# Routed experts over scattered slot tiles in DRAM in a transformer block on one Trainium2 core

## The chip, the core and the metric

The kernel runs on one NeuronCore of one Trainium2 chip. The metric is the device time of one execution in microseconds. Engines are named as the profile names them: PE is TensorE (PEld its weight loads), DVE is VectorE, ACT is ScalarE, POOL is GpSimd, SP is SyncE, whose queue issues the DMAs.

## What is computed

x has 8 sequences of 512 tokens of 128 channels, all float32. The block is attention and a mixture of experts, both on layer-normalised input and both added to x. The attention has 16 heads of 8 channels, is causal, and adds relative terms to keys and values; it isn't touched. The expert part is, cut to what matters:

```
scores = softmax(xt @ gate_w.T)                 # 4096 tokens, 8 experts
idx = top_k(scores + gate_bias, 2)
weights = scores at idx
y = 0
for e in range(8):
    gate_e = sum(where(idx == e, weights, 0))
    h = silu(xt @ w1[e].T) * (xt @ w3[e].T)     # 128 -> 128
    y = y + gate_e[:, None] * (h @ w2[e].T)
z = silu(xt @ sw1.T) * (xt @ sw3.T) @ sw2.T     # shared, 128 -> 256 -> 128
x = x + y + z
```

## The kernel before

The program of each engine is written out by hand, with semaphores between them; an engine runs its instructions strictly in their written order.

**Attention** takes two thirds of the time. It goes over 16 pieces e (group g of two sequences, row i of 128 queries; the rows of a group in the order 2, 0, 1, 3) and 8 quads of heads q in each, as units m in software-pipelined slots. Relative scores go through DRAM: rel_copy (L974) leaves them in relS, SP's put_rel (L689) writes them to w_slots, get_near (L697) reads them back skewed into the ring near, and DVE's scores_min (L1075) adds them; exp (L998), the transposes tp (L849), their copies on ACT (L987) and DVE (L1060), and the products av follow. POOL's near_probs (L791 to L799) makes the near probabilities. For each piece there follow rv (products with tv, L882), near_values, yt (transposes, L890), normalise, yb, pj and residual; store (L711) writes the result x1 to x1_dram. The last piece's rv, yt, yb and pj run in last_row, between the first steps of the expert stage; the text calls this the tail.

**The expert stage** (expert_part) has 8 chunks of 512 tokens, one for each sequence, and 10 steps in each: two shared halves and eight experts, each over all 512 tokens. A step on TensorE is hidden (L1357 and L1358: two products of 128x512 with w1 and w3 into h1_ps and h3_ps) and product for the step two before (L1367: four products of 128x128 with the tokens' hidden values hT as weights and w2 moving; eight for the shared pair). ACT's Silu (L1392) reads h1_ps, DVE's L1412 multiplies it with h3_ps into hT. DVE adds the product to acc: L1420 for the shared part, with x1, and four L1427 for an expert, scaled by the token's gate. The gates of a token that did not choose the expert are zero, and two of the eight experts are chosen for each token, so six of eight products are multiplied by zero.

During one chunk the next is prepared: normalise on ACT (L1267), four transposes on TensorE (L1275), their copy (L1282), gate scores on TensorE (L1290), and on DVE and ACT the softmax and the choice of two (gates_shift, gates_softmax, gates_pick, gates_write; about twenty small operations, each of which waits for the one before). SP loads the chunk (L1224) and stores the output of each (L1233). The weights of all ten experts come in five DMAs during attention's third group, three chunks of x1 at the start of the last piece.

## Time and profile before

| | |
|---|---|
| three timed runs | 773.13, 774.75, 775.63 us; median 774.75 |
| span of the profiled execution | 770.0 us; no other time of its own is given for it |
| granted TensorE clock, mean | 0.979 |
| busy share of the span | PE 90%, DVE 77%, ACT 67%, POOL 33% |
| attention and projections | until about 540 us |
| expert stage | from 540.1 us to the end |

A row of the groups of instructions gives the line, the engine, the operation, out<-in by name, the shape, the count, then busy time and the mean duration of one. Matmuls overlap, so the pitch between them is read from the timeline. A float32 matmul is two records, a transpose one.

### The profile page before, as it was taken

The page shows a single profiled execution, that of the slowest core. Times are in us where ns is not written, and L with a number is a line of the kernel's source. Part 1 is how long each engine was busy: PE and PEld are TensorE (multiplying, and loading weights), DVE is VectorE, ACT ScalarE, POOL GpSimd, SP SyncE. Part 2 cuts the span into 40 slices and gives each one's busy share as a digit, 9 for nine tenths or more (in the row PEclk, how much of TensorE's full clock was granted, in tenths as well). Part 3 has the DMA queues.
Part 4 walks back from the last instruction along what each step waited for, and adds up shares of the span by engine and source line. Part 5 has one row for each costly group of instructions (what it writes and reads, how often), then busy time and mean ns, then how long its engine had stood idle before and what let it go on. Part 6 is the DMA issues. An engine that isn't in the chain of part 4 may idle for free. (4 is left out here: it accounts for less than half of the span.)

```text
span 770.0 us, 27094 instructions
## 1 busy us (share of the span) xinstructions
PE 690.5 (90%) x10316; PEld 507.9 (66%) x10368; DVE 589.2 (77%) x2036; ACT 514.7 (67%) x1032; POOL 255.8 (33%) x253
## 2 busy tenths in 40 slices
PE   4687879899888899988999988988999999999997
PEld 3465657677666677766777766766666666666665
DVE  7965686788787788787888887977566776677676
ACT  3686967688797878888888998887335343443331
POOL 9443445334355534545543445533000000000000
PEclk9988989999999999999999999999999999999999
DMA  9899998689989778787778779841000000000000
GB/s 255 262 295 335 333 303 264 203 244 277 309 250 302 255 222 253 249 238 241 236 222 266 221 232 255 271 153 50 3 22 28 29 5 23 28 15 1 14 15 14
DMA packets 117839, 138.48 MB, mean 180 GB/s; under 512 B 8976, under 2 KB 86288, under 8 KB 117520
## 3 DMA queue, kind: packets, MB, share of 16 engines
q1 hardware_dynamic: 117712, 136.75, 58.6%
q8 instruction: 84, 1.38, 0.8%
q14 instruction: 43, 0.35, 0.1%
HBM read 82.26 MB, written 54.46 MB: 178 GB/s over the span
## 5 line engine op out<-in xcount | busy, mean ns | idle before, releaser
L1075 DVE CUSTOM_DVE_ANT_0 ps<-ps,near 128x128 f32<-128x128 f32 (+3 forms) x512 | 245.1, 509 | 90.5 <-PE ps L837 57.0
L998 ACT ACTIVATE work<-ps,nmin 128x128 f32<-128x128 f32 (+3 forms) x512 | 248.4, 548 | 54.2 <-DVE nmin L1075 49.4
L849 PE MATMUL ps<-ident,work 128*128 128x128 f32 x1280 | 202.6, 278 | 20.7 <-issue 11.6
L849 PEld LDWEIGHTS ps<-ident,work 128*128 128x128 f32 x1280 | 157.0, 143 | 36.5 <-issue 13.7
L795 POOL TENSOR_SCALAR_AFFINE_SELECT work<-work 128x512 f32<-128x512 f32 x96 | 61.5, 641 | 237.8 <-ACT work L987 203.6
L1392 ACT ACTIVATE near<-ps 128x512 f32<-128x512 f32 x80 | 47.5, 595 | 133.3 <-PE ps L1357 133.2
L799 POOL TENSOR_TENSOR work<-work 128x512 f32<-128x512 f32 x96 | 124.2, 1294 | 8.0
L1060 DVE COPY work<-ps 128x512 f32<-128x512 f32 (+1 forms) x192 | 123.2, 642 | 2.5 <-issue 1.6
L837 PE MATMUL ps<-kb,qb 128*128 128x384 bf16 (+3 forms) x460 | 110.6, 298 | 12.3 <-ACT work L998 9.4
L1367 PEld LDWEIGHTS ps<-work,near 128*128 128x128 f32 x640 | 82.6, 192 | 34.2 <-issue 31.6
L987 ACT ACTIVATE work<-ps 128x512 f32<-128x512 f32 (+1 forms) x160 | 90.2, 564 | 18.7 <-PE ps L849 18.1
L866 PE MATMUL ps<-work,vb 128*9 128x128 f32 x2560 | 96.1, 277 | 4.2 <-ACT relS L974 2.6
L1412 DVE TENSOR_TENSOR near<-near,ps 128x512 f32<-128x512 f32 x80 | 54.9, 687 | 50.3 <-ACT near L1392 36.4
L974 ACT ACTIVATE relS<-ps 128x512 f32<-128x512 f32 x128 | 84.4, 660 | 11.6 <-PE ps L824 10.2
L1367 PE MATMUL ps<-work,near 128*128 128x128 f32 x640 | 83.2, 275 | 0.0
L1357 PE MATMUL ps<-near,work 128*128 128x512 f32 x160 | 82.8, 599 | 0.0
L1358 PE MATMUL ps<-near,work 128*128 128x512 f32 x160 | 81.8, 593 | 0.0
L1427 DVE SCALAR_TENSOR_TENSOR near<-ps,near 128x128 f32<-128x128 f32 x256 | 71.9, 343 | 5.3
L866 PEld LDWEIGHTS ps<-work,vb 128*9 128x9 f32 x2560 | 57.7, 91 | 26.5 <-issue 19.7
L1075 DVE DVE_READ_ACCUMULATOR2_ANT nmin<- 128x1 f32 x512 | 72.1, 141 | 0.0
L882 PE MATMUL ps<-tv,work 128*32 128x8 f32 x4096 | 59.3, 179 | 12.1 <-issue 11.9
L882 PEld LDWEIGHTS ps<-tv,work 128*32 128x32 f32 x4096 | 48.2, 112 | 30.5 <-issue 27.3
(111 smaller groups left out, 627.3 us busy)
## 6 DMA issues: line engine op xcount, KB each, us to landing
near<-w_slots SPq DMA_DIRECT2D x96, 512.0 KB, 5.4
w_slots<-relS SPq DMA_DIRECT2D x128, 256.0 KB, 4.5
qk_rows<-work SPq DMA_DIRECT2D x36, 256.0 KB, 4.7
near<-w_slots SPq DMA_DIRECT2D x32, 256.0 KB, 4.6
qk_rows<-y SPq DMA_DIRECT2D x9, 256.0 KB, 6.8
qb<-qk_rows SPq DMA_DIRECT2D x24, 96.0 KB
kb<-qk_rows SPq DMA_DIRECT2D x24, 96.0 KB
qb<-qk_rows SPq DMA_DIRECT2D x48, 48.0 KB
```

What stands on the lines that cost most here:

```text
L799: nc.gpsimd.tensor_tensor(dst, ptmp[:, :, :], pT[:, q % 2, :, i * P:(i + 1) * P], ALU.add).then_inc(pc_done, 1)
L837: ins = nc.tensor.matmul(qk_ps[:, m % 3, h * wide:(h + 1) * wide], qb[:, n, i * P:(i + 1) * P], kb[:, n // 4 * 2 + n % 2, 0:wide], start=T ...
L849: ins = nc.tensor.transpose(tp_ps[:, m % 2, n * P:(n + 1) * P], prob[:, m % PROBS, n * P:(n + 1) * P], ident[:, :])
L866: ins = nc.tensor.matmul(bank[32 * h:32 * h + VD, a * P:(a + 1) * P], vb[:, g % 2, b * NI + j, n * VD:(n + 1) * VD], pT[:, q % 2, h, j * P ...
L882: ins = nc.tensor.matmul(bank[32 * tq:32 * tq + NH, a * D:(a + 1) * D], pcT[:, e % 2, tau, :], tv[:, tau, :], start=True, stop=True)
L974: nc.scalar.activation(relS[:, q % RSLOTS, :, :, :].rearrange("p a j h -> p a h j"), misc("rel", q).rearrange("p (a h j) -> p a h j", a=2, ...
L987: nc.scalar.activation(pT[:, q % 2, n * w:n * (w + 1), 0:wide], tp_ps[:, m % 2, 0:n * wide].rearrange("p (h s) -> p h s", h=n), ACT.Copy). ...
L998: ins = nc.scalar.activation(prob[:, m % PROBS, h * wide:(h + 1) * wide], qk_ps[:, m % 3, h * wide:(h + 1) * wide], ACT.Exp, bias=nmin[:, ...
L1060: nc.vector.tensor_copy(pT[:, q % 2, n * w:n * (w + 1), 0:wide], tp_ps[:, m % 2, 0:n * wide].rearrange("p (h s) -> p h s", h=n)).then_inc( ...
L1075: nc.vector.tensor_tensor_reduce(out=scores, in0=scores, in1=near[:, q % NEAR, a, 4 * P - wide:4 * P, r], scale=1.0, scalar=3e38, op0=ALU. ...
L1357: nc.tensor.matmul(h1_ps[k % 2], w1_sb[:, m, :], rhs, start=True, stop=True).then_inc(h1_ready, 1)
L1367: ins = nc.tensor.matmul(y_ps[k % 2][:, n * P:(n + 1) * P], hT[:, (NM * c + m) % 4, n * P:(n + 1) * P], w2_sb[:, m, :], start=(m == ms[0]) ...
```

## The change

The expert stage is written anew; attention itself stays. The tokens are four batches of 8 tiles (1024 tokens). For each batch DVE counts, with a scan and two small matmuls on TensorE (prefix), how many tokens go to each expert, rounds each expert's count up to whole tiles of 128 slots (gates_place), and so has the slot of each token for each of its two experts (pos) and the expert of each slot tile (emap). A batch has at most RT = 23 slot tiles, whatever the routing, so 92 are always computed, in 24 rounds of up to four (six rounds a batch, the last of three).

- GpSimd, whose program had ended with attention, scatters: 64 indirect DMAs, each of 128 normalised rows (512 B each) of a tile, into xs_dram; and later 64 gathers of the same size from ys_dram into yg. All scatters stand before all gathers in its queue.
- SP clears xs_dram before (24 DMAs of up to 256 KB in the last attention row), loads the slots of each round (load_slots), stores its products (store_slots), and stores the output at the very end.
- TensorE runs the 16 shared steps of all chunks first (FRONT = CHUNKS), with the chunks' transposes and gate scores between them, and then the 24 rounds: transposes of the slots (turn_slots), for each tile a product with w1 and w3 of its own expert, and the product with w2.
- ACT reads four experts' numbers into registers in each round and copies these experts' weights (384 columns a tile) into wbuf, and copies each product from PSUM to yo (take_product).
- DVE copies the turned slots (copy_slots), and in combine multiplies the gathered rows by the token's weight and adds them, four operations for two tiles; eight lots in steps 30 to 39, eight after the loop.
- The tail of the last piece uses one PSUM bank, and the residual comes one step sooner. Weights come in eight DMAs, chunks 2 to 5 after the last near load.

The core of the diff:

```diff
+CT = CH // P
+CHUNKS = TILES // CT
+
+BATCHES = 4
+BT = TILES // BATCHES
+RT = (TOPK * BT * P + E * (P - 1)) // P
+ROUND = 4
+ROUNDS = -(-RT // ROUND)
+NR = BATCHES * ROUNDS
+CLEARS = NR
+ZEROS = C
+RED = 3 + 2 * TOPK
+RSET = 6 * BT * E + (TOPK + 1) * BT * E + RED * BT + 7 * E + RT * (E - 1)
+NTAB = 2 * P + E * BT + RT + E
+WSETS = 4
+XGS = 6
+YOS = 3
+YGS = 4
+FRONT = CHUNKS
+SEQ = ([("shared", c, m) for c in range(FRONT) for m in range(NSH)] + [("round", r, 0) for r in range(NR)]
+       + [("shared", c, m) for c in range(FRONT, CHUNKS) for m in range(NSH)])
+NS = len(SEQ)
+ROUND_AT = NSH * FRONT
+TURN_AT = [-1, 0, 1, 2, 3, 4, 9, 10]
+GATE_AT = [0] + [at + 1 for at in TURN_AT[1:]]
+PREFIX_AT = [5, 7, 9, 15]
+PICKS_AT = [(1, 2, 2, 3, 4), (3, 4, 5, 6, 6), (5, 6, 7, 8, 8), (11, 12, 12, 13, 14)]
+COMBINE_AT = [*range(30, 34), *range(36, 40)]
...
 RSLOTS = 5
...
 PROBS = 5
-WEIGHTS = 5
+WEIGHTS = 8
 MINS = 32
...
-                        for j in range(3):
+                        for j in range(2):
+                            wait_stored(sp, j)
+                            experts["load"](sp, j)
+                    if 0 <= m - FIRST[NQ - QUADS] - 2 < CLEARS:
+                        experts["clear"](sp, m - FIRST[NQ - QUADS] - 2)
+                    if m == READ_AT[NQ - 1] + 1:
+                        for j in range(2, CHUNKS - 2):
                             wait_stored(sp, j)
                             experts["load"](sp, j)
                 load_residual(GI - 1)
...
-                        experts["pool"](pool)
+                        experts["pool_start"](pool)
                     near_probs(q)
+                experts["pool"](pool)
...
+    def clear_slots(sp, k):
+
+        sp.wait_ge(zero_done, 1)
+        g, n = divmod(k, ROUNDS)
+        a = tiles_of(k)
+        sp.dma_start(xs_dram[g][n * ROUND * P:(n * ROUND + a) * P, :].rearrange("(p a) c -> p a c", p=P),
+                     zeros.unsqueeze(1).broadcast_to([P, a, C])
+        ).then_inc(zero_out, 16)
+
     def load_tokens(sp, j):
-        sp.dma_start(x1c[j % 3], x1_tiles[:, CT * j:CT * (j + 1), :]).then_inc(x1c_in[j % 3], 16)
...
+    def load_slots(sp, r):
+
+        g, n = divmod(r, ROUNDS)
+        if n == 0:
+            sp.wait_ge(xs_out[g], 16 * TOPK * BT)
+        wait(sp, xg_ready, r - XGS + 1)
+        sp.dma_start(xg[:, r % XGS, 0:tiles_of(r), :], slot_rows(xs_dram, r)).then_inc(xg_in[r % XGS], 16)
+
+    def store_slots(sp, r):
+
+        sp.wait_ge(yo_done, r + 1)
+        sp.dma_start(slot_rows(ys_dram, r), yo[:, r % YOS, 0:tiles_of(r) * C].rearrange("p (a c) -> p a c", c=C)
+                     ).then_inc(yo_out[r % YOS], 16)
 
     def sync_program(sp, wait_stored):
+        for j in range(CHUNKS - 2, CHUNKS):
+            wait_stored(sp, j)
+            load_tokens(sp, j)
+        for r in range(XGS):
+            load_slots(sp, r)
+        for r in range(NR):
+            store_slots(sp, r)
+            if r + XGS < NR:
+                load_slots(sp, r + XGS)
         for c in range(CHUNKS):
-            if c + 3 < CHUNKS:
-                sp.wait_ge(acc_done, AC * c + 1)
-                wait_stored(sp, c + 3)
-                load_tokens(sp, c + 3)
-            sp.wait_ge(acc_done, AC * (c + 1))
-            sp.dma_start(out_tiles[:, CT * c:CT * (c + 1), :], acc[:, c % 2, :, :]).then_inc(out_done[c % 2], 16)
-        for n in range(2):
-            sp.wait_ge(out_done[n], 16 * CHUNKS // 2)
+            sp.wait_ge(comb_done, TOPK * CT * (c + 1))
+            sp.dma_start(out_tiles[:, CT * c:CT * (c + 1), :], x1c[c]).then_inc(out_done, 16)
+        sp.wait_ge(out_done, 16 * CHUNKS)
+
+    def pool_start(pool):
...
     def pool_program(pool):
-        for e in range(E):
-            ins = nc.gpsimd.memset(order[:, e:e + 1], float(E - e))
-        ins.then_inc(order_done, 1)
+        pool.wait_ge(zero_out, 16 * CLEARS)
+        for g in range(BATCHES):
+            pool.wait_ge(pos_done, g + 1)
+            pool.wait_ge(xn_done, BT // CT * (g + 1))
+            for n in range(BT):
+                for r in range(TOPK):
+                    c, m = divmod(g * BT + n, CT)
+                    nc.gpsimd.indirect_dma_start(
+                        xs_dram[g], bass.IndirectOffsetOnAxis(pos[:, g, r, n:n + 1], 0), xn[:, c, m, :], None,
+                        bounds_check=RT * P - 1, oob_is_err=False).then_inc(xs_out[g], 16)
+        for g in range(BATCHES):
+            for k in range(YOS):
+                pool.wait_ge(yo_out[k], 16 * len(range(k, ROUNDS * (g + 1), YOS)))
+            for n in range(BT):
+                lot = (g * BT + n) // 2
+                if n % 2 == 0:
+                    wait(pool, comb_done, TOPK * 2 * (lot - YGS + 1))
+                for r in range(TOPK):
+                    nc.gpsimd.indirect_dma_start(
+                        yg[:, lot % YGS, n % 2, r, :], None, ys_dram[g],
+                        bass.IndirectOffsetOnAxis(pos[:, g, r, n:n + 1], 0),
+                        bounds_check=RT * P - 1, oob_is_err=False).then_inc(yg_in[lot % YGS], 16)
...
+    def turn_slots(pe, r):
+        pe.wait_ge(xg_in[r % XGS], 16 * (r // XGS + 1))
+        wait_turned(pe, "slots", r)
+        for a in range(tiles_of(r)):
+            ins = nc.tensor.transpose(xT_ps[:, a * P:(a + 1) * P], xg[:, r % XGS, a, :], t["ident"][:, :])
+        ins.then_inc(xg_ready, 1)
...
+    def prefix(pe, g):
+
+        pe.wait_ge(count_done, g + 1)
+        pe.wait_ge(*((sh_done, 2), (sh_done, 3), (cnt_done, 2), (sh_done, 4))[g])
+        totals = routes[g % 2]["count_by_expert"][:, :, BT - 1]
+        nc.tensor.matmul(cnt_ps[:, 0:E], before, totals, start=True, stop=True)
+        nc.tensor.matmul(cnt_ps[:, E:2 * E], ones, totals, start=True, stop=True).then_inc(cnt_ready, 1)
...
+    def gates_count(dve, g):
+
+        v, then = routes[g % 2], chained(dve, g, 16)
+        pick = v["pick"]
+        then(nc.vector.tensor_tensor(v["mine_by_expert"].rearrange("p e n -> p n e"), pick[:, 0, :, :], pick[:, 1, :, :], ALU.add))
+        nc.vector.tensor_tensor_scan(v["count"], keep, v["mine"], 0.0, ALU.mult, ALU.add).then_inc(count_done, 1)
+
+    def gates_place(dve, g):
+
+        v, then = routes[g % 2], chained(dve, g, 17)
+        cnt, pad, off, tmp = v["cnt"], v["pad"], v["off"], v["tmp"]
+        dve.wait_ge(cnt_ready, g + 1)
+        nc.vector.tensor_copy(cnt, cnt_ps).then_inc(cnt_done, 1)
+        dve.wait_ge(cnt_done, g + 1)
+        then(nc.vector.tensor_scalar(pad[:, 0, :], cnt[:, E:2 * E], float(P - 1), None, ALU.add))
+        then(nc.vector.tensor_scalar(pad[:, 1, :], pad[:, 0, :], 7, 7, ALU.logical_shift_right, ALU.logical_shift_left))
+        then(nc.vector.tensor_tensor_scan(v["last"], ones[:, 0:E], pad[:, 1, :], 0.0, ALU.mult, ALU.add))
+        then(nc.vector.tensor_tensor(off[:, 0, :], cnt[:, 0:E], v["last"], ALU.add))
+        then(nc.vector.scalar_tensor_tensor(out=off[:, 1, :], in0=off[:, 0, :], scalar=-1.0,
+                                            in1=pad[:, 1, :], op0=ALU.add, op1=ALU.subtract))
+        then(nc.vector.tensor_tensor(v["rank_by_expert"], v["count_by_expert"],
+                                     off[:, 1, :].unsqueeze(2).to_broadcast([P, E, BT]), ALU.add))
+        for r in range(TOPK):
+            then(nc.vector.tensor_tensor(tmp[:, :, :], v["pick"][:, r, :, :], v["rank_by_expert"].rearrange("p e n -> p n e"),
+                                         ALU.mult))
+            with nc.allow_low_precision(reason="numbers of slots are whole"):
+                ins = nc.vector.tensor_reduce(pos[:, g, r, :], tmp[:, :, :], AX.X, ALU.add)
+            if r + 1 < TOPK:
...
+    def gates_map(dve, g):
+
+        v, then = routes[g % 2], chained(dve, g, 26)
+        wide7 = [P, RT, E - 1]
+        then(nc.vector.tensor_tensor(v["eq"], starts.unsqueeze(2).to_broadcast(wide7),
+                                     v["last"][:, 0:E - 1].unsqueeze(1).to_broadcast(wide7), ALU.is_ge))
+        with nc.allow_low_precision(reason="numbers of experts are whole"):
+            nc.vector.tensor_reduce(emap[:, g, 0:RT], v["eq"], AX.X, ALU.add).then_inc(emap_done, 1)
+        for r in range(TOPK):
+            then(nc.vector.tensor_tensor(v["tmp"][:, :, :], v["pick"][:, r, :, :], v["score"][:, :, :], ALU.mult))
...
+        def hidden(s):
+            kind, n, m = SEQ[s]
+            wait(pe, silu_done, s - 1)
+            wait(pe, hT_done, s - 1)
+            if kind == "shared":
+                pe.wait_ge(xnT_done, n + 1)
+                nc.tensor.matmul(h1_ps[s % 2], ws[:, 0, m, :], xnT[:, n, :], start=True, stop=True).then_inc(h1_ready, 1)
+                nc.tensor.matmul(h3_ps[s % 2], ws[:, 1, m, :], xnT[:, n, :], start=True, stop=True).then_inc(h3_ready, 1)
+                return
+            pe.wait_ge(xgT_done, n + 1)
+            pe.wait_ge(wbuf_done, n + 1)
+            for k, (bank, ready) in enumerate(((h1_ps, h1_ready), (h3_ps, h3_ready))):
+                for a in range(tiles_of(n)):
+                    at = slice(a * P, (a + 1) * P)
+                    ins = nc.tensor.matmul(bank[s % 2][:, at], wbuf[:, n % WSETS, a, k * P:(k + 1) * P], xgT[:, n % 2, at],
+                                           start=True, stop=True)
+                ins.then_inc(ready, 1)
+
...
+                for a in range(CT):
+                    for k in range(NSH):
+                        ins = nc.tensor.matmul(bank[:, a * P:(a + 1) * P], hT[:, (s - 1 + k) % 4, a * P:(a + 1) * P],
+                                               ws[:, 2, k, :], start=(k == 0), stop=(k == NSH - 1))
+            else:
+                for a in range(tiles_of(n)):
+                    ins = nc.tensor.matmul(bank[:, a * P:(a + 1) * P], hT[:, s % 4, a * P:(a + 1) * P],
+                                           wbuf[:, n % WSETS, a, 2 * P:3 * P], start=True, stop=True)
             ins.then_inc(y_ready, 1)
 
...
-            if k == NM * (CHUNKS - 4):
+        def copy_weights(r):
+            g, n = divmod(r, ROUNDS)
+            if n == 0:
+                act.wait_ge(emap_done, g + 1)
+            at = slice(ROUND * n, ROUND * n + tiles_of(r))
+            _, which = nc.values_load_multi_w_load_instructions(
+                emap[0:1, g, at], engines=[mybir.EngineType.Activation], min_val=0, max_val=E - 1,
+                skip_runtime_bounds_check_because="a count of seven comparisons")
+            if r >= WSETS:
+                act.wait_ge(y_ready, made(ROUND_AT + r - WSETS))
+            for a in range(tiles_of(r)):
+                ins = nc.scalar.activation(wbuf[:, r % WSETS, a, :], wr_v[:, bass.ds(which[a] * W, W)], ACT.Copy)
+            ins.then_inc(wbuf_done, 1)
+
+        def take_product(s):
+            r, p = SEQ[s][1], PRODUCTS.index(s)
+            act.wait_ge(y_ready, p + 1)
+            wait(act, yo_out[r % YOS], 16 * (r // YOS))
+            nc.scalar.activation(yo[:, r % YOS, 0:tiles_of(r) * C], y_bank(p)[:, 0:tiles_of(r) * C], ACT.Copy
+                                 ).then_inc(yo_done, 1)
...
+                cut = P * tiles_of(SEQ[s][1]) if SEQ[s][0] == "round" else CH
+                act.wait_ge(h1_ready, s + 1)
+                wait(act, hT_done, s - 1)
+                nc.scalar.activation(silu[:, s % 2, 0:cut], h1_ps[s % 2][:, 0:cut], ACT.Silu).then_inc(silu_done, 1)
+            last_row(s)
+            if s >= 2 and SEQ[s - 2][0] == "round":
+                take_product(s - 2)
+            if s + 2 < NS and SEQ[s + 2][0] == "round":
+                copy_weights(SEQ[s + 2][1])
+            for j in range(1, CHUNKS):
+                if TURN_AT[j] == s:
+                    copy_turned(act, j)
...
+        def copy_slots(r):
+            cut = P * tiles_of(r)
+            dve.wait_ge(xg_ready, r + 1)
+            if r >= 2:
+                dve.wait_ge(h3_ready, ROUND_AT + r - 1)
+            nc.vector.tensor_copy(xgT[:, r % 2, 0:cut], xT_ps[:, 0:cut]).then_inc(xgT_done, 1)
...
+        def add_shared(s):
+            c, p = SEQ[s][1], PRODUCTS.index(s)
+            dve.wait_ge(y_ready, p + 1)
+            nc.vector.tensor_tensor(x1c[c], y_bank(p).rearrange("p (n c) -> p n c", c=C), x1c[c], ALU.add).then_inc(acc_done, 1)
+
+        def combine(lot):
+            g, n = divmod(2 * lot, BT)
+            c, m = divmod(2 * lot, CT)
+            dve.wait_ge(acc_done, c + 1)
+            dve.wait_ge(yg_in[lot % YGS], 16 * 2 * TOPK * (lot // YGS + 1))
+            for r in range(TOPK):
+                for k in range(2):
+                    if r:
+                        dve.wait_ge(comb_done, 2 * TOPK * lot + k + 1)
+                    nc.vector.scalar_tensor_tensor(out=x1c[c][:, m + k, :], in0=yg[:, lot % YGS, k, r, :],
+                                                   scalar=wsel[:, g, r, n + k:n + k + 1], in1=x1c[c][:, m + k, :],
+                                                   op0=ALU.mult, op1=ALU.add).then_inc(comb_done, 1)
```

## Rows read from the trace of the kernel before

**Rows 1.** The page: busy share of each engine, and DMA by slices.

```profile
PE 690.5 (90%) x10316; PEld 507.9 (66%) x10368; DVE 589.2 (77%) x2036; ACT 514.7 (67%) x1032; POOL 255.8 (33%) x253
...
DMA  9899998689989778787778779841000000000000
```

**Rows 2.** Busy time by windows: length, then each engine, clock, DMA share, GB/s.

```profile
485.00:500.00 15.00, 14.36 (x320) 11.18 (x322) 13.47 (x45) 13.80 (x29) 8.00 (x10) 1.00 0.82 261
500.00:515.00 15.00, 12.35 (x284) 9.81 (x287) 10.68 (x33) 12.05 (x20) 4.86 (x6) 1.00 0.52 173
515.00:530.00 15.00, 14.08 (x270) 11.33 (x276) 13.88 (x42) 12.21 (x21) 5.84 (x7) 1.00 0.27 82
...
575.00:602.43 27.43, 27.43 (x134) 17.86 (x133) 20.77 (x73) 13.46 (x21) 0.00 (x0) 1.00 0.07 20
```

**Rows 3.** The page: the chain that ended last, shares by line.

```profile
PE ps L1367 9%; PE ps L1357 9%; PE ps L1358 9%; PE ps L1290 1%; PE ps L1275 1%; PE ps L882 0%; PE ps L866 0%; DVE near L1427 0%; ACT work L987 0%; PE ps L849 0%; ACT near L1267 0%; PE ps L905 0%; PE ps L890 0%; ACT work L998 0%; PE ps L837 0%
```

**Rows 4.** Timeline of TensorE within a chunk: start, length, instructions.

```profile
607.53 1.95 PE L1367 MATMUL ps<-work,near 128*128 128x128 f32 x16
609.32 0.60 PE L1275 MATMUL ps<-ident,near 128*128 128x128 f32 x4
609.75 1.02 PE L1357 MATMUL ps<-near,work 128*128 128x512 f32 x2
610.62 1.02 PE L1358 MATMUL ps<-near,work 128*128 128x512 f32 x2
611.47 1.05 PE L1367 MATMUL ps<-work,near 128*128 128x128 f32 x8
612.37 1.02 PE L1357 MATMUL ps<-near,work 128*128 128x512 f32 x2
```

**Rows 5.** Timeline: first and last matmul of the stage, last store.

```profile
540.10 1.13 PE L1357 MATMUL ps<-near,work 128*128 128x512 f32 x2
...
765.78 0.28 PE L1367 MATMUL ps<-work,near 128*128 128x128 f32 x1
767.25 0.37 SPq L1233 DMA_DIRECT2D out<-near  x1
```

**Rows 6.** Groups of instructions of ScalarE, by form.

```profile
L1392 ACT ACTIVATE near<-ps 128x512 f32<-128x512 f32 x80 | 47.5, 595 | 133.3 <-PE ps L1357 133.2
L987 ACT ACTIVATE work<-ps 128x384 f32<-128x384 f32 x64 | 32.8, 513 | 3.5 <-PE ps L849 3.5
```

**Rows 7.** Timeline of VectorE and ScalarE, 602 to 607 us.

```profile
602.28 1.12 DVE L1427 SCALAR_TENSOR_TENSOR near<-ps,near 128x128 f32<-128x128 f32 x4
...
603.53 0.19 DVE L1335 TENSOR_TENSOR near<-near 128x32 f32<-128x32 f32 x1
603.76 0.19 DVE L1336 TENSOR_TENSOR near<-near,work 128x32 f32<-128x32 f32 x1
...
605.65 1.64 ACT L1267 ACTIVATE near<-vb,work,rstd 128x128 f32<-128x128 f32 x4
```

**Rows 8.** One line's instructions: SP's output stores, issue and landing.

```profile
L1233 SPq DMA_DIRECT2D out<-near x8: 372/378/378, 578.0 to 767.2; - x8
...
DMA to landing us min/median/max: 2.3/2.3/2.9
```

**Rows 9.** The page: groups of instructions, GpSimd and VectorE at 128x512.

```profile
L795 POOL TENSOR_SCALAR_AFFINE_SELECT work<-work 128x512 f32<-128x512 f32 x96 | 61.5, 641 | 237.8 <-ACT work L987 203.6
...
L799 POOL TENSOR_TENSOR work<-work 128x512 f32<-128x512 f32 x96 | 124.2, 1294 | 8.0
L1060 DVE COPY work<-ps 128x512 f32<-128x512 f32 (+1 forms) x192 | 123.2, 642 | 2.5 <-issue 1.6
```

**Rows 10.** Timeline of SP's queue in the last attention row.

```profile
494.03 0.53 SPq L697 DMA_DIRECT2D near<-w_slots  x1
...
518.97 0.53 SPq L697 DMA_DIRECT2D near<-w_slots  x1
```

**Rows 11.** The page: DMA issues, KB each, us to landing.

```profile
near<-w_slots SPq DMA_DIRECT2D x96, 512.0 KB, 5.4
```

More of the change, by code:

```diff
@@ L9 @@
 BF16 = mybir.dt.bfloat16
+I32 = mybir.dt.int32
 ALU = mybir.AluOpType
@@ L39 @@
 CH = 512
+CT = CH // P
[25 more added lines that the diff above has]
+COMBINE_AT = [*range(30, 34), *range(36, 40)]
+TURNED = [("turn", 0)]
+for s in range(NS):
+    if s + 1 < NS and SEQ[s + 1][0] == "round":
+        TURNED.append(("slots", SEQ[s + 1][1]))
+    if s in TURN_AT:
+        TURNED.append(("turn", TURN_AT.index(s)))
+PRODUCTS = [s for s in range(NS) if SEQ[s][0] == "round" or SEQ[s][2] == NSH - 1]
 GI = G * NI
@@ L1207, in prepared_at, with tiles_of @@
-    def prepared_at(j):
-        late = LATE if j == 1 else 0
-        base = NM * (j - 1) + late
-        return {"normalise": base - late + 1, "turn": base + 2, "copy": base + 3, "scores": base + 4, "shift": base + 5,
-                "exp": base + 6, "softmax": base + 7, "pick0": base + (8 if j > 1 else 7),
-                "pick1": base + (9 if j > 1 else 8)}
-    def due(step, what):
-        return [j for j in range(1, CHUNKS) if prepared_at(j)[what] == step]
+    def tiles_of(r):
+        return min(ROUND, RT - ROUND * (r % ROUNDS))
@@ L1508, in twice @@
         return placed
-    hidden = lambda shared, experts: np.concatenate([shared.reshape(NSH, P, C), experts]).transpose(2, 0, 1)
+    tables = np.concatenate([np.broadcast_to(row, (P, row.shape[-1])) for row in (
+        np.triu(np.ones((P, P), np.float32), 1), np.ones((1, P), np.float32),
+        np.tile((np.arange(BT) > 0).astype(np.float32), E)[None], P * np.arange(RT, dtype=np.float32)[None],
+        E - np.arange(E, dtype=np.float32)[None])], axis=1)
     arrays = {
```

426 lines of the change are left out of this document (221 added, 205 removed).

## Prediction

> **What bounds the kernel now.** I read the page first: TensorE is busy for 90% of the span, more than any other engine, and in the slices the DMA engines fall nearly silent for the last 30% of the span [rows 1]. Then the busy time by windows: in the expert stage, from 540.1 us on, TensorE is busy without a gap (27.43 us of 27.43 in one chunk of ten steps) at full granted clock, with ScalarE at 13.5 us, VectorE at 20.8 us, GpSimd at nothing and DMA at 7% [rows 2]. The chain of waits says the same: its expert part is the three matmul lines alone [rows 3]. So that stage is worth what TensorE's work in it is worth, and nothing else in it is near a limit. Last I read the pitch of the matmuls from the timeline, since a matmul's own duration (593 ns) overlaps its successor's: one 128x512 product is two records and 0.855 us (611.47 less 610.62), a group of four 128x128 products with new weights each is eight records and 0.89 us (0.2225 each), the double group of a shared product 1.79, four transposes 0.43 us [rows 4]. Twenty hidden products, one shared and eight routed second products and four transposes are 17.1 + 1.79 + 7.12 + 0.43 = 26.4 us; the other 1.0 us of a chunk's 27.43 is its gate scores.
>
> The profiled execution is given with its span of 770.0 us alone; the timed runs' median of 774.75 lies 4.75 us above it. I make the sum against the span, and add 4.75.
>
> **What the change takes from TensorE.** The stage has 80 hidden steps now, and its last matmul ends at 766.1 [rows 5]: 226.0 us. Of it 80 x 1.71 = 136.8 are hidden products, 64 x 0.89 = 57.0 routed second products, 8 x 1.79 = 14.3 shared ones, 3.0 and 8.0 transposes and gate scores. The rest, 6.9 us, is the last attention row's tail (rv, yt, yb, pj) with its waits; it stays, now in one PSUM bank. Afterwards the shared part is 16 x 1.71 + 14.3 + 11.0 = 52.7, with the tail 59.6, and with eight small prefix matmuls (0.2 each) and a stall or two some 62 us. A slot tile costs three 128x128 products with new weights and a transpose: 3 x 0.2225 + 0.108 = 0.775 us, 92 tiles 71.3 us. TensorE's work falls from 226 to 133 us. That is the most that can come back, 93 us; the question is what else now takes over 133 us.
>
> **ScalarE in the rounds.** Each of 24 rounds (20 of four tiles, 4 of three) asks of it a Silu of 0.595 us and a PSUM copy of the same size; four copies of 384 columns into wbuf, 513 ns each from the nearest form [rows 6], with 0.10 us of each hidden under the next (four L1267 of 0.48 us take 1.64 us together) [rows 7]: 3 x 0.416 + 0.513 = 1.76; and a load of four expert numbers from SBUF into registers, which no row shows. Below it is nothing (behind Silu and copy); above, the shortest round trip to memory in the trace, a store's 2.3 us from issue to landing [rows 8]. I take 1.1, near the middle, since nothing says which end is nearer. A round is then 0.60 + 0.60 + 1.76 + 1.1 = 4.05 us (3.4 with three tiles), against TensorE's 3.1, so ScalarE sets the pace: 20 x 4.05 + 4 x 3.4 = 94.6 us. With the ends it is 3.1 (TensorE's) to 5.3. VectorE needs 0.64 us for copy_slots [rows 9], about as much for the gated product and at most 1.12 for a combine a round [rows 7] and is covered. TensorE at three quarters busy should keep its clock: the window 500 to 515, 82% busy, has 1.00 [rows 2].
>
> **GpSimd's queue.** It is idle now from 541 on. It gets 64 scatters and then 64 gathers, each of 128 rows of 512 B, one instruction each, strictly in order. None is in the trace. Bound from below: SP hands a DMA out in 0.38 us [rows 8]. Above: 2.3 us, if each held the queue until it landed. GpSimd's own 128x512 instructions take 0.64 to 1.29 us [rows 9]. With 128 addresses to work out I take 1.2 us, near GpSimd's dearer instruction and below the landing. The Trainium skill, "DMA: Bandwidth & Descriptors", section "Anatomy of one DMA", gives a GpSimd-issued DMA about 2.0 us fixed, most of it the completion, not the setup. Held in the queue for the whole of it, 128 would be 256 us and the span some 833; no row here shows which part holds the queue.
>
> When can it start? The first batch's positions come after the prefix at step 5. Steps 0 to 4 cost TensorE 5 x 1.71 + 1.79 + 5 x 1.25 = 16.6 us plus some 6 of the tail, step 5 some 4, then eleven chained VectorE operations at 0.225 us each (603.53 to 603.76) [rows 7]: 30 us after 540.1. The chain of 36 such operations a batch is 8.1 us, 32 for four; with 16 gated products, 8 additions (0.65 to 0.7 each) and some 4 us of tail that is 53 of the 62 us, so covered, if closely. Scatters run from 30 to 30 + 64 x 1.2 = 107; batch 0's land at about 52, before the first round's transposes at 58. Gathers of the first three batches follow without a gap (their rounds are stored by 97, 121, 145), and the last 16 start at 164.
>
> **The sum.** Last round: 62 + 94.6 + 3 for the two steps behind = 160; stored and landed 2.7 later, 162.3. GpSimd comes free for the last batch at 30 + 112 x 1.2 = 164.4, so its queue decides, by 2 us. Sixteen gathers, 19.2: 183.6. Behind the last: 2.3 to land, 1.12 for its four VectorE products, 0.4 and 2.3 for the last store: 6.1, so 189.7. 540.1 + 189.7 = 729.8.
>
> **The clears and the loads.** SP issues 24 clears of 256 KB during the last attention row, 493 to some 527, 6 MB where the DMA engines are 82, 52 and 27% busy [rows 2]. Five near loads (512 KB, 5.4 us to landing) go out between them in SP's queue, the last at 518.97 [rows 10, 11], and VectorE's scores wait for those, ScalarE's exp for VectorE, TensorE's transposes for that. The idle DMA share of 493 to 527 is some 17 us' worth of all engines; 5.9 MB at 261 / 0.82 = 318 GB/s is 19. So some contention is left: I take 1 us, with nothing and 6 us as ends (nothing, if the loads stay ahead; 6, if all five land 1.2 us late, one clear's issue and transfer each). Weights go from five DMAs to eight, of 0.4 to 0.5 us on SP, some 0.2 MB more, spread over 14 units two rows earlier: on a queue whose DMAs wait for ScalarE's rel copies anyway: nothing. Chunks 2 to 5 are loaded at once behind the last near load, under the end of attention; the two last chunks behind the last store as now. The batched gate takes four exponentials and their table loads from ScalarE, which is not what sets the end there. Span 731, time **736 us**, 5% faster.
>
> **Rivals.**
> - *The last gathers are cheap and registers too (faster still).* At 0.9 us a DMA and 3.4 us a round: 62 + 80 + 3 + 2.7 + 14.4 + 6.1 = 168, 713 us. For it: a 64 KB DMA is little work. With both lower ends, 0.38 and 3.1, it is 151, 696 us.
> - *GpSimd's queue is the bound and eats the gain (slower).* The end is 540.1 + 30 + 128c + 6.1 + 1, equal to today's 770 at c = 1.51 us. At 1.75 it is 801, 806 us; at 2.3 it is 872, 876. For it: 128 rows need 128 addresses each way and the queue is serial; GpSimd needs 1.29 us for one tensor addition [rows 9]. Against: SP's 0.38. This is the rival that ends on the other side, and one price decides it.
> - *Register loads hold ScalarE.* The end is 62 + 24 x r + 3 + 2.7 + 19.2 + 6.1 + 1, equal to today's at r = 5.7 us a round, a load of 2.7 us; four single loads in a row would do that. At 6.5 us a round it is 790, 795 us. The Trainium skill, "DMA: Bandwidth & Descriptors", section "Latency and other measured facts", gives a register load a floor of about 600 ns; by that a round would be 3.6 us and the sum, set by GpSimd, the same.
> - *VectorE locks GpSimd out.* If every copy_slots (0.64 us) held the descriptors back, 24 of them would add 15 us: 751 us. The Trainium skill, "SBUF — State Buffer", has this for fp32 copies from SBUF to SBUF in a fast mode. Against: these read PSUM, and L1060's 512 columns from PSUM take 0.642 us [rows 9], so no fast mode shows.
>
> **Chances.** Forecast (722 to 755 us) 0.50, with VectorE's lock in it; both cheap 0.15; GpSimd over 1.5 us a DMA 0.21; registers 0.08; something between, near no change or a little under, 0.06. The break-even is only a quarter above my price for a DMA that no row shows, so the range must reach over: 708 (0.8 us a DMA, 3.3 a round) to 800 (1.7 us a DMA); the likeliest case alone 722 to 755. Faster by over 0.3% 0.69, within 0.3% (about what a measurement of this kernel can tell from no change) 0.03, slower 0.28.
>
> **What would show it.** TensorE busy some 135 us behind 540, not 226. Rounds at an even pitch of some 4.05 us, with ScalarE named before TensorE's hidden products (wbuf); at 3.1 the register load is hidden. On GpSimd 128 DMAs at a pitch of 1.2 us, the first some 570, with no gap between scatter and gather but at batch ends. The last 16 gathers with TensorE silent for 20 to 25 us at the end. Attention's end within 2 us of where it was. Wrong it would be by a pitch over 1.5 us on GpSimd, by ScalarE rounds over 5.7 us, or by near loads that land late.

## The result, and the profile of the changed kernel

The changed kernel takes 828.72 us (median of 4 runs, 825.82 to 837.52), the kernel before 773.94 in runs beside it: ratio 1.074, 95% interval 1.066 to 1.081. Forecast were 736 us and a range of 708 to 800; the prediction was wrong. The same kernel, unaltered, ran again later, on chip 3, with the experiments below: 753.86 us (two runs) against 771.44 there, ratio 0.976 (0.966 to 0.985). Both are results of this change. Most of this text is about what lies between them.

The page of the first run, for rows 1 and 3 (engines, slices, then the chain by engine):

```profile
PE 633.3 (77%) x10260; PEld 493.0 (60%) x10260; DVE 528.0 (64%) x1820; ACT 533.5 (65%) x1098; POOL 383.9 (47%) x374
...
PEclk9988899999999999999999999999758869796955
DMA  9899998799997797786877989901231024353352
...
another core or an unknown queue 10%; PE 7%; DVE 5%; issue 4%; ACT 3%; POOL 1%; DMA 1%; POOLq 0%; ACTq 0%; DVEq 0%
```

TensorE's work has fallen as meant, 690.5 to 633.3 us [rows 1], but the span has grown to 825.5 and the first name in the chain is no engine of the kernel: a release that the profile can't place. This is one core, so there is no other core to wait for. Its windows, for rows 2 (length, busy of PE, PEld, DVE, ACT, POOL, then clock, DMA share, GB/s):

```profile
500.00:515.00 15.00, 14.10 (x294) 10.63 (x291) 11.72 (x37) 13.01 (x21) 4.73 (x5) 1.00 1.07 322
515.00:530.00 15.00, 14.66 (x269) 11.56 (x268) 13.18 (x38) 12.07 (x21) 5.79 (x6) 1.00 1.06 306
575.00:602.43 27.43, 11.63 (x50) 7.17 (x48) 13.90 (x55) 8.32 (x13) 20.73 (x23) 0.75 0.34 103
```

The clears fill the DMA engines (share 1.07), and TensorE is as busy there as before: 14.10 and 14.66 us of 15, against 12.35 and 14.08. Behind the first scatter, which starts at 574.05, it is busy for 11.63 us of 27.43, at a mean granted clock of 0.75. The timeline of all engines shows why:

```profile
587.62 0.22 DVE L1485 TENSOR_REDUCE near<-near 128x8 f32<-128x64 f32 x1 [0.21 <-DVE near L1535]
589.02 0.23 DVE L1486 TENSOR_TENSOR near<-near 128x64 f32<-128x64 f32 x1 [1.18 <-DVE near L1485]
589.72 0.23 DVE L1487 TENSOR_TENSOR near<-near,work 128x64 f32<-128x64 f32 x1 [0.47 <-DVE near L1486]
...
603.22 1.09 PE L1405 MATMUL ps<-ident,near 128*128 128x128 f32 x4
604.10 1.92 PE L1544 MATMUL ps<-near,work 128*128 128x512 f32 x2
605.81 1.18 PE L1545 MATMUL ps<-near,work 128*128 128x512 f32 x2
613.87 0.97 POOL L1350 DMA_INDIRECT xs_dram<-near  x1 [0.30 <-issue]
619.12 0.69 DVE L1661 TENSOR_TENSOR relS<-ps,relS 128x512 f32<-128x512 f32 x1 [17.34 <-remote]
619.24 0.60 ACT L1410 ACTIVATE near<-ps 128x512 f32<-128x512 f32 x1 [32.38 <-remote]
```

L1410 copies what L1405's four transposes wrote. They end at 604.3; the copy starts at 619.24. In between ScalarE does nothing, and nothing else that the copy needs is under way. So 14.9 us of its 32.38 idle are a late signal; the rest is before the transposes ended. VectorE's chained operations wait only on VectorE's own signals, and stand 0.7 to 1.4 us apart where they took 0.23 [rows 7]. No instruction of ScalarE or VectorE got longer (0.60, 0.69, 0.22 us as ever); TensorE's did only with the clock (1.92 us for L1544's two where 1.02 is usual). I read it as a late signal from one instruction to the next. GpSimd's line in the same stretch is a run of scatters 1.28 us apart; its last begins at 613.87, and 4.4 us after that ends (614.8) the waiters go.

### The profile page after: what moved, and what is told of

The parts are those of the page before. It is cut to its first block and busy times, and to the rows that moved or that the text cites. A ratio compares the mean times of both kernels' runs of the same rounds, so it can differ in the third digit from the quotient of the medians.

```text
span 825.5 us, 27095 instructions
## 1 busy us (share of the span) xinstructions
PE 633.3 (77%) x10260; PEld 493.0 (60%) x10260; DVE 528.0 (64%) x1820; ACT 533.5 (65%) x1098; POOL 383.9 (47%) x374
## 5 line engine op out<-in xcount | busy, mean ns | idle before, releaser
L880 PE MATMUL ps<-kb,qb 128*128 128x128 bf16 (+3 forms) x512 | 130.8, 307 | 11.9 <-ACT work L1036 9.0
L1361 POOL DMA_INDIRECT work<-ys_dram,near x64 | 66.1, 1033 | 75.9 <-DMA ys_dram<-work 25.4
L1025 ACT ACTIVATE work<-ps 128x512 f32<-128x512 f32 (+1 forms) x160 | 90.4, 565 | 15.5 <-PE ps L892 14.9
L1350 POOL DMA_INDIRECT xs_dram<-near x64 | 62.4, 976 | 69.7 <-DVE near L1520 51.2
L1012 ACT ACTIVATE relS<-ps 128x512 f32<-128x512 f32 x128 | 84.3, 660 | 11.1 <-PE ps L867 9.5
L1552 PE MATMUL ps<-kb,qb 128*128 128x128 f32 x368 | 54.2, 308 | 40.0 <-DVE kb L1647 23.5
L1552 PEld LDWEIGHTS ps<-kb,qb 128*128 128x128 f32 x368 | 49.8, 217 | 43.9 <-issue 43.0
L925 PE MATMUL ps<-tv,work 128*32 128x8 f32 x4096 | 58.7, 179 | 11.6 <-issue 11.5
L1647 DVE COPY kb<-ps 128x512 f32<-128x512 f32 (+1 forms) x24 | 16.0, 668 | 78.1 <-remote 41.2
L880 PEld LDWEIGHTS ps<-kb,qb 128*128 128x128 bf16 x512 | 40.5, 98 | 31.9 <-ACT work L1036 16.2
L867 PE MATMUL ps<-te,qb 128*128 128x128 bf16 x512 | 50.5, 222 | 6.2 <-ACT relS L1012 5.5
```

The costliest lines, as they stand in the source:

```text
L880: ins = nc.tensor.matmul(qk_ps[:, m % 3, h * wide:(h + 1) * wide], qb[:, n, i * P:(i + 1) * P], kb[:, n // 4 * 2 + n % 2, 0:wide], start=T ...
L925: ins = nc.tensor.matmul(bank[32 * tq:32 * tq + NH, a * D:(a + 1) * D], pcT[:, e % 2, tau, :], tv[:, tau, :], start=True, stop=True)
L1012: nc.scalar.activation(relS[:, q % RSLOTS, :, :, :].rearrange("p a j h -> p a h j"), misc("rel", q).rearrange("p (a h j) -> p a h j", a=2, ...
L1025: nc.scalar.activation(pT[:, q % 2, n * w:n * (w + 1), 0:wide], tp_ps[:, m % 2, 0:n * wide].rearrange("p (h s) -> p h s", h=n), ACT.Copy). ...
L1361: nc.gpsimd.indirect_dma_start(yg[:, lot % YGS, n % 2, r, :], None, ys_dram[g], bass.IndirectOffsetOnAxis(pos[:, g, r, n:n + 1], 0), bound ...
L1552: ins = nc.tensor.matmul(bank[s % 2][:, at], wbuf[:, n % WSETS, a, k * P:(k + 1) * P], xgT[:, n % 2, at], start=True, stop=True)
```

## Experiments

Each ran beside the kernel before, on one chip for each group of runs. The runs name the chip: 10 for the first four, 11 for the second four, then 0, 3 and 8, in this order of time. The first result above has no chip named. "Remote" is the profile's word for a wait whose release it can't place. The kernel before has some too, 14 of at most 1.8 us in attention (11.9 us in all); what is said of remote waits below is of the expert stage.

**Without any DMA of GpSimd.** The loops of L1350 and L1361 are gone; the combine reads zeros.

> The changed kernel with all 128 DMAs of GpSimd left out (no scatter, no gather: the slot tiles hold the zeros of the clears, the combine reads zeros; the output is not the reference's). Slot loads wait for the clears and for shared step 12 alone. Theory A (the DMAs that GpSimd issues back to back hold back the other engines' signals): with them gone, the 16 shared steps run from 540 in about 62 us, the 24 rounds follow at the undisturbed pitch of 3.45 us (83 us), the combine and stores add about 12: span 695 to 715. Rival B (the rounds themselves are dear: a register load on ScalarE, 368-column copies, PE's many small matmuls): rounds stay above 4.5 us and the span is above 740. Rival C (the slot loads and stores on SP's queue are the wait): the waits on xg loads stay and the span is above 780.

Measured: 713.55 us, ratio 0.928 (0.921 to 0.934), no remote wait. The span, 710.8, lies in Theory A's range; rivals B and C fall. With all 24 rounds in it, the rest of the change is worth 58 us.

**A probe in the kernel before.** Behind GpSimd's last attention work, from step 5 of the expert stage:

```
+        for n in range(64):
+            nc.gpsimd.indirect_dma_start(flat[:, n * P:(n + 1) * P], None, rows,
+                bass.IndirectOffsetOnAxis(at, 0), ...).then_inc(probe_in, 16)
```

> The kernel before, with 64 indirect gathers of 128 rows of 512 bytes added on GpSimd, from step 5 of the expert stage on, back to back, to an unused part of the work tile; nothing waits for them. Theory A: after some ten of them the expert steps of TensorE, ScalarE and VectorE pause until the burst of about 64 x 1.3 = 83 us has ended: 30 to 75 us slower than before, with idle time put down to a remote or unknown releaser. Rival (the wait comes from the changed kernel's own order of work, or from slot traffic): within 3 us of before, since the idle GpSimd has 190 us for it.

Measured: 845.57 us against 771.51, ratio 1.099 (1.092 to 1.107). ScalarE's timeline:

```profile
611.53 0.60 ACT L1406 ACTIVATE near<-ps 128x512 f32<-128x512 f32 x1 [18.57 <-remote]
662.63 0.60 ACT L1406 ACTIVATE near<-ps 128x512 f32<-128x512 f32 x1 [50.50 <-remote]
664.17 0.60 ACT L1406 ACTIVATE near<-ps 128x512 f32<-128x512 f32 x1 [0.95 <-remote]
```

The gathers run from 574.0 to 657.4. ScalarE's instruction at 662.63 reads what this product wrote, in TensorE's timeline:

```profile
619.10 1.92 PE L1371 MATMUL ps<-near,work 128*128 128x512 f32 x2
```

It ended at 621.0, 41.6 us before its reader started. Nothing in the kernel waits for the probe, and yet it costs 74 of the 83 us that it lasts. A lack of instructions is an unlikely cause: the two queues that the profile calls instruction moved no packet between 600 and 664, so ScalarE's instruction at 662.63 hadn't just been fetched.

**The same with plain DMAs.** `dma_start(flat[...], rows[0:P, :])`, also 64 KB and from GpSimd.

> The same probe with 64 plain 64 KB loads issued by GpSimd instead of indirect ones. If issuing from GpSimd in itself (its software queue) is what holds signals back, 20 to 75 us slower than before; if it takes the indirection, within 3 us of before.

Measured: 773.74 us, ratio 1.000 (0.995 to 1.004), on the same chip. They stand 0.53 us apart. So issuing from GpSimd isn't enough; of these two it takes the indirect form.

**The changed kernel, spaced.** Two waited memsets behind each indirect DMA:

```
+                    for _ in range(2):
+                        nc.gpsimd.memset(zeros, 0.0).then_inc(zero_done, 1)
+                        spent[0] += 1
+                        pool.wait_ge(zero_done, spent[0])
```

> The changed kernel with two waited memsets of 128 x 128 on GpSimd behind each of its 128 DMAs, which should widen their pitch from 1.28 to about 1.9 us. Theory A with a backlog (signals pass when the DMAs come slower than they are served, some 1.4 us each): the pauses of 12 to 32 us vanish, rounds run at 3.5 to 4 us, and the end is set by GpSimd's own queue, 574 + 128 x 1.9 = 817 and about 15 behind it: span 820 to 850. Theory A without a threshold (any run of such DMAs holds signals back until it pauses): the pauses grow with the queue, span above 880.

Measured: 876.14 us, ratio 1.139. The pitch came out at 2.25 us, (864.8 - 579.2) / 127, not 1.9, and there is no remote wait in the trace, on the chip on which the probe had 119 us of them. So the pauses vanished, as the theory with a backlog had it, and the span of 875.9 came out above its 820 to 850, because the pitch did; the sum below explains it.

**Pitch, rows, bursts, payload.** Four variants of the probe: one waited memset behind each; 32 rows in place of 128; a wait for all landings after each eight; rows of 64 bytes.

> The probe of 64 indirect gathers in the kernel before, with one waited memset of 128 x 128 behind each, which should set their pitch at about 1.75 us (574 to 686). Backlog theory (each such DMA leaves work behind GpSimd that takes about as long as, or a little longer than, its 1.3 us of issue, and signals pass once it is given time): nearly no loss, under 10 us over before. Theory without a threshold (each DMA costs the other engines some 1.2 us of held signals whatever its pitch): again 60 to 85 us over before.

> 64 indirect gathers of 32 rows instead of 128, back to back. If the held signals come from the number of descriptors (rows), the loss is under 15 us, and the issue time shows how much of the 1.0 us on GpSimd is for the rows and how much is fixed; if it is the indirect DMA as such, the loss is the length of the burst again, over 40 us.

> The probe of 64 indirect gathers in bursts of 8, GpSimd waiting after each burst until all of it has landed (about 2 us). Backlog theory: signals are held only within a burst and pass at its end, so single pauses stay under 10 us and the loss is under 30 us where the unbroken burst lost 74. Without a backlog that empties in those 2 us the loss is 60 us or more.

> 64 indirect gathers of 128 rows of 64 bytes instead of 512, back to back: an eighth of the payload with the same descriptors. If the payload's traffic holds the signals, the loss falls under 15 us; if the descriptors do, it stays at 60 to 85 us over before.

| | pitch, us | time, us | ratio |
|---|---|---|---|
| one memset | 2.00 | 772.80 | 0.999 (0.995 to 1.004) |
| 32 rows | 1.22 | 846.67 | 1.096 (1.084 to 1.107) |
| bursts of 8 | 1.30, then a 2.2 us pause | 786.77 | 1.018 (1.007 to 1.030) |
| 64 bytes a row | 1.30 | 850.74 | 1.101 (1.089 to 1.113) |

Neither the number of rows nor the payload matters: 32 rows cost GpSimd 0.91 us against 1.00 and hold the others as long. The pauses between DMAs do: at 2.00 us nothing is lost. Bursts of eight lose about 14. Between 1.30 and 2.00 us no pitch was tried, and each pause came with a wait of GpSimd (on a memset, or on landings), so distance and wait aren't told apart. There is no run of this changed kernel at 1.3 us on chips 10 or 11.

**The changed kernel at that pitch, and without its gathers.**

> The changed kernel with one waited memset behind each of its 128 indirect DMAs, so that they stand 2.0 us apart, the pitch at which the probe lost nothing. If the held signals were all that made the change slow, the span comes near 713 plus a few us. If the queue itself then bounds, its last gather ends at about 574 + 128 x 2.0 = 830 and the span is 838 to 850, with TensorE no longer waiting on remote releasers but on slot loads and on the combine.

Measured: 838.58 us, ratio 1.087, on chip 0; the queue's end is the bound, as the second sentence had it. As no run on that chip showed late signals, paced or not, this one doesn't test whether the pitch protects from them.

> The changed kernel without its 64 gathers (the combine reads zeros, so the output is not the reference's); the scatters stand back to back as before. Backlog theory: the pauses of 12 to 17 us up to 677 stay, the rounds after them run undisturbed at 3.45 us, span 740 to 765, so that scatters and gathers cost about 40 and 70 us of the 115 over the run without either. If the scatters are harmless and only gathers hurt, the span is within 8 us of 713.

Measured: 709.20 us, ratio 0.920 (0.912 to 0.927). By its number this is the second expectation, harmless scatters. But in the first trace signals were late while scatters alone ran, so neither reading fits both: here the 64 scatters stand in one unbroken run of 82 us at 1.28 us, at the same point of the same program as in the first trace, and no signal is late. My backlog theory had no room for this. What differed was the program behind that point, or the chip.

**The same programs on one chip.**

> The changed kernel unaltered, beside the three runs below on one chip. Its first trace shows pauses of 12 to 32 us on remote releasers from the twelfth scatter on; the run without gathers, on another chip, shows none in the same instructions up to that point. If the chip makes the difference, this run goes with the other three: all four with such pauses (828 us here) or none (about 765 to 790 here). If the programs do, it is 820 to 840 with pauses while the next but one has none.

> The kernel before with 64 indirect gathers back to back, once more. If the chip makes the difference it follows the changed kernel: 845 us where that shows pauses, near the kernel before where it doesn't. If the programs do, 845 us again whatever the others show.

> The changed kernel without its gathers, once more (the combine reads zeros, the output is not the reference's). If the programs make the difference, 709 us again with no remote waits though its 64 scatters stand in an unbroken run of 82 us; if the chip does and this is one that holds signals, 735 to 765.

Measured, on chip 3: 753.86, 771.52 (ratio 1.000, 0.995 to 1.004) and 710.40 us. No remote wait in the expert stage of any. The changed kernel came out under even the 765 to 790 expected of it without pauses. The probe's windows on chip 10, and then on chip 3:

```profile
600.00:620.00 20.00, 5.21 (x14) 2.86 (x13) 1.81 (x5) 0.60 (x1) 15.15 (x16) 0.59 0.16 49
640.00:660.00 20.00, 0.00 (x0) 0.00 (x0) 0.00 (x0) 0.00 (x0) 13.40 (x14) 0.50 0.15 46
```

```profile
600.00:620.00 20.00, 20.00 (x98) 13.09 (x97) 13.75 (x45) 6.08 (x13) 15.16 (x16) 1.00 0.25 77
640.00:660.00 20.00, 20.00 (x98) 13.07 (x97) 15.11 (x54) 8.48 (x12) 13.28 (x14) 1.00 0.17 55
```

One program, the same 14 to 16 DMAs on GpSimd in each stretch, and TensorE at nothing (and half clock) or at everything. The program alone isn't the cause; the chip, or a state that it was in, decides. The changed kernel on chip 3, one window of the rounds:

```profile
640.00:700.00 60.00, 57.73 (x484) 54.95 (x483) 28.75 (x61) 47.85 (x105) 45.98 (x47) 1.00 0.69 197
```

Its scatters and gathers (lengths in ns, then first and last start; then what GpSimd waited for ahead of the gathers, us and times):

```profile
L1350 POOL DMA_INDIRECT xs_dram<-near x64: 971/972/1209, 576.2 to 656.9; - x64
...
L1361 POOL DMA_INDIRECT work<-ys_dram,near x64: 992/997/1082, 658.2 to 740.8; - x64
its engine sat idle before it (us, times) until:
  issue: 17.7, 58
  DMA ys_dram<-work: 0.9, 3
  DVE relS L1672: 0.9, 3
```

And TensorE's last round, in its timeline:

```profile
699.97 1.58 PE L1552 MATMUL ps<-kb,qb 128*128 128x128 f32 x12
```

TensorE's last round starts at 699.97; the gathers go on to 741.8 and the span ends at 751.3. GpSimd waits for others for less than 3 us from 576.2 on (1.8 ahead of gathers, 0.3 ahead of scatters). Its queue is the bound here.

**Half of the tokens dense.** What the runs pointed to: take half of the DMAs away, and put dense work where GpSimd was waited for. Batches 0 and 1 stay with slot tiles (12 rounds, 32 scatters, 32 gathers), the chunks of batches 2 and 3 go through all eight experts, and these steps stand around the rounds:

```
+MIX = "D" * 8 + "RRDRRDRRDD" + "RRDRRDRRD" + "D" * 17
+            if kind == "dense":
+                rhs = xnT[:, n, :]
...
+                nc.tensor.matmul(h1_ps[s % 2], wr_v[:, m * W:m * W + P], rhs, ...)
+                nc.tensor.matmul(h3_ps[s % 2], wr_v[:, m * W + P:m * W + 2 * P], rhs, ...)
...
+                nc.vector.scalar_tensor_tensor(out=x1c[c][:, a, :], in0=y[:, a, :], scalar=routes[g % 2]["lg"][:, n + a, e:e + 1],
+                                               in1=x1c[c][:, a, :], ...)
```

> A mixture: routed experts over slot tiles for the first half of the tokens alone (32 scatters and 32 gathers, 12 rounds), all eight experts on all rows for the other half as before the change (32 dense steps), these placed around the rounds, and the indirect DMAs 2.0 us apart. Work of TensorE: 62 us for the shared steps, 32 x 2.7 = 86, 12 x 3.45 = 41, so an end near 540 + 189 = 729; the queue ends near 574 + 32 x 2.0, then 650 + 32 x 2.0 = 716, in front of that. Span 725 to 740, some 40 us under the kernel before. If held signals need more than this pitch, or if the queue's waits land in VectorE's order, 750 or more.

> The same mixture with its indirect DMAs back to back (1.3 us apart) in bursts of 16 to 32. Backlog theory: the 32 scatters hold signals from about the tenth on and cost 10 to 30 us, the gathers in two bursts of 16 another 5 to 15: span 745 to 775, 15 to 45 us over the paced one. If pacing doesn't matter, the two are within 3 us.

Measured on chip 0: paced 735.19 us, ratio 0.954 (0.945 to 0.962); unpaced 738.59, ratio 0.959 (0.953 to 0.964); the 745 to 775 that the backlog theory gave the unpaced one didn't come. The unpaced one on chip 3, beside the changed kernel:

> The half-and-half mixture without pacing, once more: 738 us if the programs make the difference or if this chip holds no signals; 750 to 780, with remote waits in the bursts, if the chip does and holds them.

737.35 us, ratio 0.954, where the changed kernel had 753.86. Once more both, on chip 8:

> The half-and-half mixture with its indirect DMAs 2.0 us apart, on another chip. If the chip is one on which runs of indirect DMAs hold signals back, pacing should still keep it at 730 to 740, since the probe at this pitch lost nothing on such a chip; if pacing protects nothing here, 750 to 780 with remote waits.

> The same mixture unpaced beside it, as its own sign of the chip: about 738 without remote waits on a chip that holds no signals; on one that does, remote waits from about the tenth DMA of its run of 32 scatters and of its two runs of 16 gathers, and 750 to 790.

737.67 us, ratio 0.953 (0.947 to 0.959), and 737.91, ratio 0.956 (0.948 to 0.964). None of the five shows a remote wait in the expert stage. Where both ran on one chip, paced and unpaced don't differ beyond what their runs do. The paced one's windows on chip 0:

```profile
600.00:650.00 50.00, 49.54 (x301) 37.30 (x300) 27.47 (x65) 22.97 (x47) 17.16 (x30) 1.00 0.28 85
650.00:700.00 50.00, 49.33 (x302) 37.43 (x301) 31.68 (x84) 23.41 (x47) 27.44 (x45) 1.00 0.36 103
```

TensorE is full again and sets the end, at 730.0 against a forecast sum of 729. That match is luck: the expert stage of this execution began at 532.4, not at 540, so it took 8 us more than the sum. This mixture is faster than the kernel before (by 4.1 to 4.7%) and than the changed one on the better of its chips. No run of it fell on a chip that holds signals, so that pacing protects it there is argued from the probe at 2.00 us, not shown.

## Why the prediction was wrong

**The step that failed** is "The sum". It costs each DMA of GpSimd at what it takes of GpSimd, 128 x 1.2 = 154 us from the first scatter on, and lets all else run beside it. In the first result each run of them also held back the other engines, which GpSimd then had to wait for, and the same stretch took 241 us. That the queue comes last was named rightly, and so it was in all four runs of the full change. The span ends 10.5 us behind the start of the last gather in the first result (815.0, 825.5), 10.5 on chip 3 (740.8, 751.3), 10.9 and 11.1 in the spaced ones (827.2, 838.1; 864.8, 875.9). What differs is how the queue got there. GpSimd's groups in the first run:

```profile
L1361 POOL DMA_INDIRECT work<-ys_dram,near x64 | 66.1, 1033 | 75.9 <-DMA ys_dram<-work 25.4 <-DVE vb L1672 21.4 <-issue 17.7
L1350 POOL DMA_INDIRECT xs_dram<-near x64 | 62.4, 976 | 69.7 <-DVE near L1520 51.2 <-issue 18.6
L1552 PE MATMUL ps<-kb,qb 128*128 128x128 f32 x368 | 54.2, 308 | 40.0 <-DVE kb L1647 23.5 <-issue 13.9 <-ACT qb L1608 1.8
L1608 ACT ACTIVATE qb<-work 128x384 f32 x92 | 40.5, 512 | 1.1 <-issue 1.0
```

and its waits on unplaced releasers:

```profile
DVE kb L1647 <- remote: 41.2, 6, 11.6
ACT work L1615 <- remote: 33.9, 7, 11.4
ACT near L1410 <- remote: 32.4, 1, 32.4
ACT qb L1623 <- remote: 30.0, 5, 14.8
DVE relS L1661 <- remote: 22.9, 2, 17.3
```

From its first scatter (574.1) to its last gather (815.0) are 240.9 us. 127 steps at 1.29 us are 164. The rest is waiting: 19.0 us for the later batches' positions (L1520's 51.2, less the 32.2 before the first scatter), 25.4 for stored rounds, 21.4 and 11.5 for the combine; with these, 241. So the loss goes round in a circle: GpSimd's runs delay the routing and the rounds, GpSimd then waits for those, and the queue ends 74 us later than on chip 3 (815.0, 740.8). That the DMAs hold the signals back is shown by the probe (845.57 against 771.51 us) and by the run without them (713.55); this account of the circle is read from the trace of one execution.

**Point by point, by the run without late signals** on chip 3, span 751.3 against the 731 of the forecast.
- *Price of an indirect DMA* 1.2 us: 1.296, (740.8 - 576.2) / 127, scatter and gather nearly alike: 0.97 or 1.00 us busy and 0.30 between. That is +12 us. The rival's formula, with its break-even of 1.51, is 6 to 11 us short: it gives 743 at 1.296 us, 832 at 1.99 and 865 at 2.25, measured were 751.3, 838.1 and 875.9. An estimate from the first two of these runs puts the break-even near 1.45. The Trainium skill, "DMA: Bandwidth & Descriptors", section "Anatomy of one DMA", has some 2.0 us fixed for such a DMA, most of it completion. The trace agrees with the size, as the scatters landed after 2.2 us (median). But the queue moved on every 1.3, so the prediction's 833 us for a full hold falls.
- *First scatter* at 570: 576.2, +6, of it 2.8 because the stage began at 542.91. In the first run it began at 540.80 and the scatters at 574.1.
- *Tail* behind the last gather's end 6.1 us: 9.5, +3.4. The three add to 21 us, the whole of the 20 missing and the 1 us of the clears.
- *The queue decides, "by 2 us"*: by about 14. The last store was issued at 704.7 and stores landed after 2.6 us (median), and the last batch's gathers began at 721.3. The other path came out right by luck: 72.8 us to the first slot transposes (615.7) where the sum had 62, then 88.4 us to the end of the last product (704.1) where it had 97.6.
- *ScalarE's round* of 4.05 us: wrong, and harmless. Undisturbed rounds come every 3.44 us (646.25, 649.79, 653.23, 656.68), TensorE is busy for 57.73 us of 60 and ScalarE for 47.85, so TensorE sets them. Its 3.1 us was 0.34 short. The four copies are 512 ns each as foretold; the register load, which no row shows by itself, is hidden in what ScalarE has free, 12.15 us in 17.4 rounds or about 0.7 us each, and the 1.1 us that the sum gave it is too much. TensorE's work from 540 on is 148 us by the windows, not 133, and most of that is in the rounds (83 us from 615.3 on against 71.3); with the queue as the bound it cost nothing.
- *Clears*, 1 us: the stage began at 540.80 against 540.10 in the first run, and at 536.5 to 545.9 in the seven traces that have all 24 clears. So nothing speaks against 1 us, and none of these runs can show it. A DMA share of 1.07 left nothing spare.
- *VectorE locks GpSimd out*: on chip 3 the gathers, which run beside the rounds and their copy_slots, take 0.99 to 1.08 us each, and the whole queue moves every 1.3. 15 us of lock-outs would show in that. It fell.
- *GpSimd bound, slower*: right sign, wrong mechanism. At 1.3 us it doesn't decide against the change; it needed some 1.45 to 1.51.

**What is open.** Which part of the chip holds the signals back, and what sets one chip, or one hour, apart from another. Late signals showed in the first result and on chips 10 and 11; on chips 0, 3 and 8 there was none in ten traces, seven of them of unpaced runs. Every run with late signals was also earlier in time than every run on 0, 3 and 8, so the hour, or something changed on the machine in between, explains it as well as the chip does. The kernel before took 770 to 774 us on all, so it gives no sign of either. The probe ran on chips 10 and 3, the changed kernel in the first result and on 3, and no chip is known to have been tried twice.

## What to carry to other kernels

A serial queue needs its own line in the sum: 128 indirect DMAs at 1.3 us are about 166 us, and fewer rows or bytes in each didn't make it much shorter. Sending half of the tokens through it, while TensorE keeps the dense rest, took the time on chip 3 from 753.86 to 737.35 us. Time a kernel with runs of indirect DMAs on more than one chip, and at more than one hour, before it is called faster or slower: this one was 7.4% slower the first time and 2.4% faster later. Where the trace shows waits on no known releaser, compare the end of the work waited for with the start of the waiter, and look at what another engine was doing all the while.

## What the hardware showed that I hadn't expected

In some sessions (the first result, chips 10 and 11), runs of indirect DMAs at 1.2 to 1.3 us put off the signals between TensorE, ScalarE and VectorE by up to 42 us (product ended at 621.0, its reader started at 662.63), while the instructions of ScalarE and VectorE stay as long as they were; at 2.00 us on chip 11, or with plain DMAs at 0.53 us on chip 10, nothing is put off. An indirect DMA costs GpSimd nearly the same for 32 rows (0.91 us) as for 128 (1.00), and the same for 64 bytes a row as for 512. TensorE's granted clock fell to 0.50 of full (1.2 of 2.4 GHz) in the stretch in which it got no work (640 to 660 us of the probe).
